# Moving the first block of a feed-forward phase ahead of the last state sums of the phase before it

## The reference, cut to what matters

```
x = x + 0.5 * ffn(layernorm(x))
x = x + mamba(layernorm(x))
x = x + 0.5 * ffn(layernorm(x))

ffn:   h = x @ gate_w[e];  u = x @ up_w[e]                    # 16 experts, and 2 shared ones
       routed = sum_e combine[t, e] * (silu(h) * u) @ down_w[e]
       combine: sigmoid scores + bias, best 2 of 4 groups, best 4 experts, weights over their sum
mamba: dA = exp(delta * A[n]);  dBu = delta * B[n] * u        # 16 states n
       state[n](t) = dA * state[n](t-1) + dBu
       y = sum_n C[n] * state[n] + D * u;  out = concat(y, z) @ W_out
```

## Time and profile before

| | |
|---|---|
| profiled execution, whole time | 912.01 us |
| its span of records | 910.2 us |
| median of the runs | 912.05 us |
| PE busy | 868.7 us (95%) |
| DVE busy | 729.9 us (80%) |
| POOL busy | 650.8 us (71%) |
| ACT busy | 540.2 us (59%) |
| TensorE clock granted, mean | 0.994 of full |

### The profile page before, as it was taken

One profiled execution on the slowest core, in us unless ns is written; L12 is line 12 of the kernel. 1 busy time (PEld: TensorE's weight loads), 2 busy tenths in 40 slices (PEclk: granted clock), 3 DMA queues, 4 the chain that ended last, 5 costly groups with the idle time before them and its releaser, 6 DMA issues. The chain is left out here.

```text
span 910.2 us, 12224 instructions
## 1 busy us (share of the span) xinstructions
PE 868.7 (95%) x3591; PEld 621.9 (68%) x3591; DVE 729.9 (80%) x1257; ACT 540.2 (59%) x951; POOL 650.8 (71%) x476
## 2 busy tenths in 40 slices
PE   8999999999999998999999977799999999999997
PEld 7777778877767775455445433477787788788885
DVE  4989878877975567999999989978896787696664
ACT  7565565565554668767776574246556556555554
POOL 7758776766756567898898877846576677676765
PEclk9999999999999999999999998999999999999999
DMA  8715374353343342444344443251627545545450
GB/s 205 222 53 157 125 203 122 113 152 128 94 138 108 91 122 97 151 142 154 133 151 161 131 144 120 80 159 47 182 76 197 157 132 150 158 112 162 152 128 23
DMA packets 120611, 121.33 MB, mean 133 GB/s; under 512 B 55001, under 2 KB 78689, under 8 KB 120545
## 3 DMA queue, kind: packets, MB, share of 16 engines
q1 hardware_dynamic: 102352, 116.35, 42.4%
q10 hardware_dynamic: 18192, 4.21, 2.1%
HBM read 111.87 MB, written 8.65 MB: 132 GB/s over the span
## 5 line engine op out<-in xcount | busy, mean ns | idle before, releaser
L714 POOL TENSOR_TENSOR act_lo<-act,act_hi 128x512 fp32r<-128x512 f32 x288 | 372.3, 1297 | 208.5 <-ACT act_hi L827 208.3
L820 ACT ACTIVATE bank<-bank 128x512 f32<-128x512 f32 x252 | 146.6, 582 | 239.3 <-PE bank L1155 220.3
L1051 DVE TENSOR_TENSOR sg<-bank,c_ring 128x512 f32<-128x512 f32 x252 | 172.2, 683 | 95.0 <-ACT bank L820 88.2
L1151 PE MATMUL bank<-x_parts,w_hi 128*128 128x512 f32 x572 | 234.4, 410 | 10.2 <-DVE act L1029 7.5
L1029 DVE SCALAR_TENSOR_TENSOR act<-sg,bank 128x512 f32<-128x512 f32 x288 | 197.8, 687 | 38.6 <-PE bank L1155 20.7
L1155 PE MATMUL bank<-x_parts,w_hi 128*128 128x512 f32 x572 | 225.8, 395 | 0.0
L1152 PE MATMUL bank<-x_parts,w_lo 128*128 128x512 f32 x572 | 225.6, 394 | 0.0
L827 ACT ACTIVATE act_hi<-act 128x512 fp32r<-128x512 f32 x288 | 179.3, 623 | 1.0 <-PE bank L1127 0.8
L1151 PEld LDWEIGHTS bank<-x_parts,w_hi 128*128 128x128 f32 x572 | 107.6, 188 | 48.3 <-DVE act L1029 16.5
L1152 PEld LDWEIGHTS bank<-x_parts,w_lo 128*128 128x128 f32 x572 | 107.7, 188 | 25.5 <-issue 2.6
L1155 PEld LDWEIGHTS bank<-x_parts,w_hi 128*128 128x128 f32 x572 | 107.6, 188 | 25.5
(11 more groups left out here) (177 smaller groups left out, 992.3 us busy)
## 6 DMA issues: line engine op xcount, KB each, us to landing
c_ring<-c_dram SPq DMA_DIRECT2D x252, 256.0 KB, 3.8
c_ring<-c_dram SPq DMA_DIRECT2D x64, 512.0 KB, 3.6
y_dram<-out_t SPq DMA_DIRECT2D x56, 64.0 KB, 2.9
y_tok<-y_dram SPq DMA_DIRECT2D x14, 256.0 KB, 3.7
xt_dram<-xn ACTq DMA_DIRECT2D x32, 64.0 KB, 3.6
xt<-xt_dram ACTq DMA_DIRECT2D x8, 256.0 KB, 3.3
out<-x_sb SPq DMA_DIRECT2D x7, 256.0 KB, 2.3
x_sb<-in_L_attn_hidden_states SPq DMA_DIRECT2D x3, 512.0 KB, 6.1
```

Source lines behind the costliest of these rows:

```text
L714: self.nc.gpsimd.tensor_tensor(m["act_lo"][:, g % LAG], m["act"][:, g % ACTS], m["act_hi"][:, g % LAG].bitcast(FP32), ALU.subtract).then_i ...
L820: nc.scalar.activation(self.s_bank[:, g % 2], self.h_bank[:, g % 2], ACT.Silu).then_inc(self.sg_ready, 1)
L1051: nc.vector.tensor_tensor(m["sg"][:, g % 2], silu, weight, ALU.mult).then_inc(self.w_done, 1)
L1151: nc.tensor.matmul(dst, m["w_hi"][:, k, n, :], x_hi, start=True, stop=False)
```

## The change

The first block of `f2` gets its products in `acc` (h) and `misc` (u) instead of `h_bank` and `u_bank`. PE's order becomes: block 0, sum of pair 61, block 1, sum of pair 62, block 2, logits of row 1, sum of pair 63, block 3, projection. Block 0 waits for the routing of row 0 (`comb_ready`) and no longer for scans; block 1 takes over those waits. DVE copies `y_acc` behind its part of block 1 and adds the projection to `x_sb` behind its part of block 2, each one block later than before. In the last row of the state-space phase POOL adds no pairs, and PE sums both states of all eight.

```diff
@@ dve stream
                 tail = mamba.dve_tail(dve)
                 for g, _ in enumerate(f2.dve_blocks(dve)):
-                    if g < 2:
+                    if g in (1, 2):
                         next(tail)
@@ pe stream
                 tail = mamba.pe_tail(pe)
-                next(tail)
                 for g, _ in enumerate(f2.pe_blocks(pe)):
-                    if g == 0:
-                        next(tail)
-                        next(tail)
-                    if g == 1:
+                    if g < SUM_LAG + 1:
                         next(tail)
@@ class Ffn
+    def h_dst(self, g):
+        return self.acc if self.mamba and g == 0 else self.h_bank[:, g % 2]
+
+    def u_dst(self, g):
+        return self.misc if self.mamba and g == 0 else self.u_bank[:, g % 2]
@@ act_blocks
-                    nc.scalar.activation(m["sg"][:, g % 2], self.h_bank[:, g % 2], ACT.Silu
+                    nc.scalar.activation(m["sg"][:, g % 2], self.h_dst(g), ACT.Silu
@@ dve_act
-                                            self.u_bank[:, g % 2], ALU.mult, ALU.mult).then_inc(self.act_ready, 1)
+                                            self.u_dst(g), ALU.mult, ALU.mult).then_inc(self.act_ready, 1)
@@ pe_blocks
                 if self.mamba and g == 0:
+                    pe.wait_ge(self.comb_ready, 1)
+                if self.mamba and g == 1:
                     pe.wait_ge(self.mamba.scan_done, ALL_PAIRS - 1)
                 need(pe, self.sg_ready, g - 1)
-                self.pe_product(pe, self.h_bank[:, g % 2], 0, g).then_inc(self.h_ready, 1)
+                self.pe_product(pe, self.h_dst(g), 0, g).then_inc(self.h_ready, 1)
...
                 if self.mamba and g == 0:
+                    self.onto_misc(pe, self.act_ready, 1)
+                if self.mamba and g == 1:
                     pe.wait_ge(self.mamba.scan_done, ALL_PAIRS)
                 need(pe, self.act_ready, g - 1)
-                self.pe_product(pe, self.u_bank[:, g % 2], 1, g).then_inc(self.u_ready, 1)
+                self.pe_product(pe, self.u_dst(g), 1, g).then_inc(self.u_ready, 1)
@@ pool_pairs
-                if n in ADDED:
+                if n in ADDED and i < BATCH - 1:
@@ pe_add_states
-        for s in range(1 if n in ADDED else 2):
+        for s in range(1 if n in ADDED and i < BATCH - 1 else 2):
```

## The result

The changed kernel takes 914.8 us (median of 12 runs, 912.65 to 916.57) against 912.03 us (12 runs, 909.38 to 914.27): a ratio of 1.0033, 95% interval 1.0023 to 1.0043. It is 2.8 us slower; 913.2 was forecast, and the range ended at 914.4. The profiled execution took 914.51 us with a span of 912.8.

A forecast was written before the change was run, and what follows sets the result against it. DVE was taken to set the pace in blocks 3 to 9; 0.25 us from the later add plus 0.95 from the collision, +1.2 us on the profiled 912.01, gave 913.2 us, range 911.0 to 914.4.

The forecast's parts named there:

- where PE's head start ends: At block 3, PE is 1.2 us ahead, but the silu waits for DVE's add of the projection: 0.25 us late.
- the collision: Before block 4, three POOL subtractions without a pause hold DVE's two-operand routing instructions; `sg` of block 4 1.2 us late.
- the delay is carried whole: From `act` of block 4, ACT, POOL and PE follow DVE as before, so 1.2 us lasts to the end.
- Rival 3: PE's granted clock falls to half in a slice of 584 to 597 us, costing 2 us more: 915.3; chance 0.08.
- POOL's part: Dropping POOL's adds frees 3 x 1.27 us, but PE asks for the last product 2 us after it: nothing gained or lost.
- units of 3.15: PE's time for one pair's sum of four passes plus a block of six, taken between 3.09 and 3.20 us.

The follow-up runs named there:

- Experiment 1: Changed kernel with GpSimd's subtractions for blocks 2 and 3 held back until VectorE's second and third routing pieces were issued; 912.13 us, ratio 0.9994 to the kernel before.
- experiment 3: Changed kernel, but GpSimd adds pairs 1, 5 and 6 of the last state-space row again; 911.93 us, ratio 1.0001 to the kernel before.
- run 10: One more profiled execution, for the clock, of the changed kernel with GpSimd's adds of pairs restored; two such executions took 908.49 and 910.8 us.
- experiment 6: Kernel before with only the GpSimd part of the change, no pairs added in the last state-space row; 911.37 us, ratio 0.9991 to the kernel before.
- experiment 4: Changed kernel unaltered, measured again; 914.7 us, ratio 1.0025 to the kernel before.
- experiment 7: Changed kernel with pairs added again, subtractions held back and row 1's first routing piece ahead of block 3; 909.11 us, ratio 0.9969 to the kernel before.

## Why the prediction was wrong

**Right: where PE's head start ends.** PE had no idle time between 584 and 601 us. The silu of block 3 ended its wait on the add. The add started 12.40 us from the mark, where the sum has 12.37 (598.98 - 586.61). From the mark the silu started at 13.18 us where it had been 12.81: 0.37 late, in the forecast 0.0 to 0.45 and near the 0.25 taken. The change from the old wait to the new one is as forecast.

**Right: the collision.** Three subtractions without a pause (3.79 us), `pair_sum` at 2.53, `sg` of block 4 at 18.91 us from the mark in place of 17.57: 1.34 late where 1.2 was forecast. The second of the three `pair_sum` instructions lost to the third subtraction, as its 0.03 us of lateness had it. Taken by itself, that second one started at 603.19 and took 1.31 us. The rule of the page SBUF — State Buffer in the Trainium skill, section "Who interferes with whom", that whoever issues first keeps the shared pair for the whole instruction, holds in the numbers of these runs. Experiment 1 shows the cause and not only the place.

**Wrong: "From `act` of block 4 on, ACT, POOL and PE (u of block 6 waits for it) follow it as before, so the delay is carried whole".** They did not follow as before, since PE had come early. Its idle time in front of u of block 6 went from 0.67 to 2.75 us, while the change removed its earlier gaps. I had both numbers: the head start of 1.2 us and the delay of 1.2 us, and 0.67 + 1.2 + 1.2 = 3.1 us of gap follows from them. (Measured, the head start is 1.2 at block 4 and 0.74 by the end of h of block 6, and the delay 1.34: 0.67 + 0.74 + 1.34 = 2.75.) I did not add them up, because a PE that waits for DVE seemed to cost nothing. Behind the gap PE ran at half the clock, and the price in the end was 1.65 us: the sum was 0.25 + 0.95 and lacked this term. With it the forecast would have been 914.85. But the 1.65 could not have been had from the length of the slow stretch alone: that is 1.54, and it is near the end result only because the stall that it swallowed (at 616.85) and the one that it brought about (at 630.42) nearly cancel.

**Rival 3 had the mechanism at the wrong place.** It put the fall of the clock into 584 to 597 us, where PE is busy without a pause, and rightly found nothing for it there; it should have been asked of the stretch in which the change makes PE wait longer. That its 915.3 is near the measured 914.8 is luck. The rule of the page TensorE: Matmul & The Clock Gate of the Trainium skill, Part 1, that the throttled state is the default and activity releases it, was used to keep the chance of it small; read at 604 to 608 us, with PE busy 1.35 of 4 us, it speaks for a fall, and the trace agrees there. In experiment 3 it would speak for one just as much (1.76 of 4 us busy in the same window, 1.26 of 4 in run 10), and there was none.

**POOL's part** was priced at nothing gained and nothing lost. In the old order that is so (experiment 6). In the new one it is 1.4 us of the add's start, which my sum held in its units of 3.15 without naming it: each unit carries four passes of a sum. Only the sums of pairs 61 and 62 have these passes more. It was a cost of this part, not of the order.

**Open:** why the clock falls behind the gap of the changed kernel and not behind one of the same length in experiment 3. The two differ in where the gap lies (17.6 and 16.2 us from the mark it begins) and in what PE did before it. Four falls in four profiles and none in three are hardly chance from run to run (one way in 35 of spreading four falls over seven profiles), and the medians of experiments 3 and 4 are 2.8 us apart, about what the passes and the fall make together; what makes the difference no run shows.

## What to carry to other kernels

Where a faster engine is made to wait for another one, work out its new idle time, the old one plus head start plus delay, and ask what the clock does behind it: here a TensorE that was off the path came back onto it with half the clock. What such a stretch costs in the end is read at a later stall, since the delay swallows one wait and can bring about another. Before an engine's idle gap is filled, ask what else it was hiding, here the passes that GpSimd's adds saved, and a pause of GpSimd in which VectorE's two-operand instructions passed. Such a collision moves when its parts move (line 925 in experiment 1, lines 941 and 945 behind the slow stretch), and in experiment 7 it took both: a wait on the side that has slack, and one of the other side's pieces put where the first was idle anyway.

## What the runs showed of the hardware that I had not expected

VectorE's `tensor_scalar` with one operand in SBUF and 16 columns was held by GpSimd's subtraction as well: 1.24 us in experiments 1 and 7, against 0.18 in the changed kernel (line 923 there), where it started as GpSimd's subtraction was 0.14 us from its end. I had counted only instructions with two SBUF operands as exposed. And a gap of TensorE of 2.73 to 2.75 us was followed by half the clock in all four profiles of one kernel, and in none of three of another that differs from it by six passes ahead of the gap, whose work GpSimd does there.
